# Expert work spread over the quads of a recurrent scan by a table of shares instead of evenly

## The reference, cut to what matters

```python
def step(h, inp):                      # branch s: a scan over 1024 steps
    dAt, dBt, xt, Ct = inp
    h = dAt * h + dBt * xt[..., None]
    h_norm = jnp.sqrt(jnp.sum(h * h, axis=(1, 2), keepdims=True))
    scale = jnp.minimum(20.0 / (h_norm + 1e-08), 1.0)
    h = h * scale
    y = jnp.einsum('bdn,bn->bd', h, Ct) + Dp * xt
    return (h, y)
...
exp_batches = jnp.einsum('tec,td->ecd', sec_mask, xt)      # branch f: 8 experts, top 2 of 8, 1280 slots each
h = jax.nn.gelu(jnp.einsum('ecd,edf->ecf', exp_batches, c_fc), approximate=False)
exp_out = jnp.einsum('ecf,efd->ecd', h, c_proj)
out = cb_weight.reshape(T, N_EXP * cap) @ exp_out.reshape(N_EXP * cap, d)
```

## Time and profile before

| | |
|---|---|
| median of 3 runs | 1628.38 us (1627.27 to 1630.05) |
| the profiled execution: its own time | 1631.96 us |
| its span in the profile | 1630.2 us |
| busy: PE, DVE, ACT, POOL | 79%, 93%, 71%, 47% |
| mean granted TensorE clock | 0.892 |
| expert work runs in | about 304 to 1420 us of the span |

### The profile page before, as it was taken

The page is one execution under the profiler, slowest core; times in us unless marked ns, Lnnn a source line. Parts: engine busy times, 40 slices in busy tenths (PEclk is TensorE's granted clock), DMA queues, the critical chain, the costliest instruction groups (busy, mean ns, idle before and its releaser), DMA issues.

```text
span 1630.2 us, 34378 instructions
## 1 busy us (share of the span) xinstructions
PE 1280.4 (79%) x9628; PEld 1121.2 (69%) x9628; DVE 1519.3 (93%) x9635; ACT 1161.4 (71%) x2944; POOL 770.5 (47%) x1254
## 2 busy tenths in 40 slices
PE   5665535689899888989989997999989798945661
PEld 4555434578788777878878786888878688734550
DVE  6888888999999999999999999999999999987788
ACT  7887647577786868777776877778777767846550
POOL 4267767444444443444443344344444434468852
PEclk9767767799999999999989999999999999978795
DMA  9921111201120020120012002101201100012255
GB/s 342 320 74 48 46 41 43 96 18 30 38 73 24 18 74 24 37 74 24 24 42 69 17 30 67 37 31 35 64 16 28 66 28 18 18 42 71 72 160 186
DMA packets 85088, 104.56 MB, mean 64 GB/s; under 512 B 7712, under 2 KB 75936, under 8 KB 84896
## 3 DMA queue, kind: packets, MB, share of 16 engines
q1 hardware_dynamic: 76848, 85.47, 16.2%
q0 software_dynamic: 6144, 16.79, 3.2%
q10 hardware_dynamic: 1904, 0.09, 0.1%
HBM read 56.45 MB, written 45.88 MB: 63 GB/s over the span
## 4 chain that ended last, share of the span: by engine, by line
PE 49%; POOL 15%; ACT 15%; DVE 11%; issue 8%; DMA 2%; POOLq 0%; SPq 0%; ACTq 0%; DVEq 0%
PE ps L1277 16%; PE ps L1261 13%; PE ps L1249 8%; POOL arena L520 7%; PE ps L1243 5%; POOL xg L503 4%; ACT arena L891 4%; PE ps L1211 2%; DVE arena L694 2%; ACT arena L1008 2%; DVE arena L720 2%; DVE arena L740 2%; POOL wf L509 2%; DVE arena L730 2%; POOL wp L509 2%
## 5 line engine op out<-in xcount | busy, mean ns | idle before, releaser
L520 POOL TENSOR_TENSOR arena<-arena,neghalf 128x1 f32<-128x1 f32 x1025 | 594.6, 580 | 791.5 <-DVE arena L684 786.7
L694 DVE SCALAR_TENSOR_TENSOR arena<-arena 128x128 f32<-128x128 f32 x1024 | 363.4, 355 | 23.3 <-POOL arena L520 23.3
L1249 PE MATMUL ps<-arena,pick 128*128 128x128 f32 x2048 | 299.9, 293 | 63.2 <-ACT arena L1008 39.7
L1249 PEld LDWEIGHTS ps<-arena,pick 128*128 128x128 f32 x2048 | 276.5, 209 | 77.1 <-ACT arena L1008 64.4
L1261 PE MATMUL ps<-arena,wf 128*128 128x256 f32 x1280 | 306.8, 391 | 22.5 <-ACT arena L1023 10.4
L1008 ACT ACTIVATE arena<-ps,arena 128x128 f32<-128x128 f32 x1024 | 292.3, 374 | 29.6 <-PE ps L1249 27.8
L1277 PE MATMUL ps<-wp,arena 128*128 128x256 f32 x1280 | 303.7, 392 | 9.0 <-ACT arena L1023 5.9
L730 DVE CUSTOM_DVE_ANT_0 arena<-arena 128x128 f32<-128x128 f32 x1024 | 293.0, 286 | 12.2 <-ACT arena L1008 8.9
L720 DVE CUSTOM_DVE_ANT_0 arena<-arena 128x128 f32<-128x128 f32 x1024 | 298.5, 291 | 2.2
L689 DVE TENSOR_TENSOR arena<-arena 128x128 f32<-128x128 f32 x1024 | 289.4, 283 | 0.0
L1261 PEld LDWEIGHTS ps<-arena,wf 128*128 128x128 f32 x1280 | 243.2, 197 | 54.9 <-ACT arena L1023 11.2
(11 more groups left out here) (148 smaller groups left out, 1329.1 us busy)
## 6 DMA issues: line engine op xcount, KB each, us to landing
xg<-zeros SPq DMA_DIRECT2D x10, 1024.0 KB, 10.9
xrow<-xg SPq DMA_DIRECT2D x40, 256.0 KB, 2.8
yg<-arena SPq DMA_DIRECT2D x40, 256.0 KB, 2.2
arena<-in_x SPq DMA_DIRECT2D x16, 512.0 KB, 9.1
wf<-in_c_fc SPq DMA_DIRECT2D x8, 1024.0 KB, 5.3
wp<-in_c_proj SPq DMA_DIRECT2D x8, 1024.0 KB, 6.1
ys<-arena SPq DMA_DIRECT2D x66, 64.0 KB, 1.6
xnd<-arena SPq DMA_DIRECT2D x8, 512.0 KB, 6.8
```

Source lines behind the costliest of these rows:

```text
L520: g.tensor_tensor(sv[:, slot, 1:2], mx, neghalf[:, 0:1], ALU.pow).then_inc(s_ready, 1)
L694: v.scalar_tensor_tensor(hr[:, slot, :], vv, sv[:, before, 1:2], ur[:, slot, :], ALU.mult, ALU.add).then_inc(h_ready, 1)
L1249: last = t.matmul(ps[2][:, j * P:(j + 1) * P], pick[:, q * QUAD + j, :], xin, start=True, stop=True)
```

## The change

Each quad from 41 to 229 gets a share ("room"): 0.8 in a half's last quad (15), 0.3 in its first (0), 0.7 in the second (1), 0.9 in the third (2) and fifth (4), and 1.0 elsewhere. The item list is the same, in the same order; an item goes to the first quad at which the accumulated room exceeds the item's middle, in units. The sixteen shares of a half add up to 14.6, so a quad of share 1.0 is meant to get 16/14.6 of the even load.

```diff
+import itertools
...
         QUADS, MOE_AT, MOE_QUADS, COMBINE_AT, LAST_HALF = NT // QUAD, 41, 230, 237, 240
+        share = {15: 0.8, 0: 0.3, 1: 0.7, 2: 0.9, 4: 0.9}
+        room = [share.get(qd % 16, 1.0) if MOE_AT <= qd < MOE_QUADS else 0.0 for qd in range(QUADS)]
+        ends = list(itertools.accumulate(room))
         n = 0
         total = sum(w[3] for w in work)
         by_quad = [[] for _ in range(QUADS)]
         for w in work:
-            by_quad[MOE_AT + (n + w[3] // 2) * (MOE_QUADS - MOE_AT) // total].append(w)
+            by_quad[next(qd for qd in range(QUADS) if ends[qd] > (n + w[3] / 2) / total * ends[-1])].append(w)
             n += w[3]
```

## The result

The changed kernel takes **1656.33 us** (1645.62 to 1657.55, five runs) against 1630.05 us (1627.27 to 1633.14) for the one before beside it: ratio 1.0154, 95% interval 1.0125 to 1.0183. It is slower, as forecast, but by 26 us where some 8 were forecast, and outside the range. The latter is called the longer profile, the former the shorter one.

What follows compares the result with a forecast made beforehand. VectorE's scan was taken as bound by a slower feeding chain of TensorE and ScalarE, 11.2 us of waits. Terms: -23.9 + 34.2 - 5.5 + 2.6 - 1.6 + 1.8 = +7.6 us on 1628.4, so 1636 us; range 1620 to 1644 us.

Steps and rivals of the forecast that it cites:

- The feeding chain: TensorE's matmuls for a quad, ScalarE's eviction, the next quad; feeds VectorE's scan, slower than it by 19.7 us.
- three stretches: Each half's last two, first two and other twelve quads, summed over halves 3 to 13: together 1038.3 us before.
- First two quads: Start of each half, 154 units to 80: down to ScalarE's floor, 189.2 to 165.3 us, -23.9.
- Last two quads: End of each half, 150 units to 151: -1.6 us against 160.4.
- a unit's price in busy time: A unit is the item list's weight; 0.444 us each, 77 more in the twelve quads +34.2 us.
- the twelve quads: Quads 2 to 13 of halves 3 to 13, bounded by TensorE: 925 units to 1002, from 688.8 to about 720 us.
- Rival (a): Faster: TensorE's gaps in the twelve quads swallow most of the moved work, 0.17 us a unit, 1620 us; chance 0.26.
- a quarter of the 22.6, -5.5: Twelve quads: a quarter of TensorE's 22.6 us of idle time there takes up moved work, -5.5 us.
- rival (c): Start of a half: TensorE idles a second time and its clock falls, +9 to +12 us, 1646 us; chance 0.1.
- The second idle time: TensorE waits up to 4 us for the second quad's L1008, the first quad being empty.
- the table loads, +2.6: Second to fourth quad: four more ScalarE table loads of 1.28 us, half of 5.1 us on the path.
- nearly every microsecond ... is a microsecond of the kernel: Lead is never large again after half 3, so changes to the stretches' sum change the kernel's time nearly one for one.

Runs made afterwards that it cites:

- longer profile: Profile of an execution of the changed kernel run again without any edit: 1657.13 us.
- shorter profile: Profile of the changed kernel's first measurement, the fastest of its five executions: 1645.62 us.
- e2_first_two: Kernel before with only the shares of a half's first and second quad (0.3 and 0.7): 1652.96 us, ratio 1.0131.
- e3_last: Kernel before with only the share of a half's last quad (0.8): 1632.15 us, ratio 1.001.
- e4_more_first: Kernel before with more work at a half's start, share 1.5 in its first quad and 1.3 in its second: 1650.12 us, ratio 1.0104.
- e12_less_work: Changed kernel with 76 units of expert work left out of quads 2 to 13 of halves 3 to 13: 1634.21 us, ratio 1.0026 to before.
- e7_one_table: Changed kernel with the Gelu's table, which holds tanh too, loaded after each half's Ln, 37 loads instead of 47: 1654.55 us, ratio 1.0144 to before.
- e11_other_three: Kernel before with only the shares of a half's last (0.8), third and fifth quad (0.9): 1625.37 us, ratio 0.9982.

## Why the prediction missed

**Right: the mechanism and two of its three stretches.** The feeding chain bounds, its sum of three stretches moves the time (12.2 us of sum for 13.7 of time in the first profile, 24.1 for 25.2 in the longer one), and the work went from quads where it is partly free to quads where TensorE is full. First two quads: forecast 165.3, measured 163.25 and 164.65. Half 5, forecast about 18, took 18.76, half 13, forecast 15.3, 14.45. Last two quads: forecast -1.6, measured -1.5 and +0.2. VectorE's waits for quads: forecast 19 in all, measured 23.5, most of them for a half's second quad, as forecast, and 34.6 in the longer profile.

**Right: a unit's price in busy time.** What the twelve quads gained or lost against before, in us, split into TensorE's busy time at full clock, the cost of the lower clock (half of the change of the busy time at 1.2 GHz) and idle time:

| run | units | stretch | busy, full clock | a unit | lower clock | idle |
|---|---|---|---|---|---|---|
| changed, shorter profile | +77 | +39.6 | +34.2 | 0.44 | +3.4 | +2.1 |
| changed, longer profile | +77 | +48.4 | +33.6 | 0.44 | +13.2 | +1.6 |
| e2_first_two | +53 | +31.1 | +23.6 | 0.44 | +5.7 | +1.8 |
| e3_last | +16 | +1.5 | +6.3 | 0.39 | -2.4 | -2.3 |
| e4_more_first | -41 | -8.8 | -16.5 | 0.40 | +3.3 | +4.4 |

The forecast was 34.2 for 77 units, and e12_less_work gives the same 0.44. Rival (a) fell with it. The Trainium skill, "Perfetto Trace Analysis", section "Identifying the Most-Contended Engine", would judge TensorE's headroom by weight loads (and by the share of its peak rate), not by matmul busy time. Weight loads were busy 629.5 of 728.4 us, 86%, and the trace disagrees with the rule here: a unit cost its full price all the same. What is added to the price, or taken off, is clock and idle time: in e3_last both fell, and 16 units more lengthened the stretch by only 1.5 us.

**Wrong: "a quarter of the 22.6, -5.5".** Idle time in the twelve quads went from 22.6 to 24.7 and 24.2 us. The prediction read the gaps as mostly those behind quads with little work, where ScalarE is slower. By what ended it, the idle time before is 11.7 us for the copy of the transposed inputs (L952), 3.8 for the late weight load, 3.5 for ScalarE's input terms (L1008), 2.7 for nothing that the profile shows and 0.9 for the copy of turned rows (L1027). Only the 3.5 are of the kind that the prediction meant. They were filled, down to 0.8 in the longer profile; the first two and the fourth stayed (11.4, 3.9, 2.7). New ones came in their place: 3.0 us in which a "down" waits for a Gelu, and 2.2 instead of 0.9 for the copy of turned rows.

**Wrong: the clock priced as rival (c), chance 0.1, "at 2.9 us in three or four halves".** It is part of the usual execution. The second idle time was seen, but expected where an "up" alone stands in the second quad (halves 4, 7, 9). It came in 7 and 9, not in 4, and also in halves 8 and 11, with a "down" there, and 12, with two "up"s, since with the first quad empty ScalarE's chain ended after TensorE's work there too. The lower clock in the twelve quads costs 3.4 us more than before in the shorter profile and 13.2 in the longer one, whose time the other runs share (1654 to 1658 us). The prediction's sum has no term for it. The twelve quads, forecast +31.3 with the table loads: in the longer profile 34.2 for units, 13.2 for the clock and 1.6 of idle time make 49.0, measured 48.4. The two failed terms, 13.2 and 5.5 + 1.6, are 20.3 us; the change cost 26.3 us against 7.6 forecast, 18.7 more.

**Mis-sized: the table loads, +2.6.** e7_one_table puts ten loads at 2.0 us, so four at about 0.8, an estimate. The Trainium skill, "ScalarE: Activation LUTs", section "What ACT_TABLE_LOAD costs", would give ten switches an estimated 26.6 us of ScalarE's time. The trace agrees with its figure for the load, 1.28 us, but shows no drain: ScalarE stood idle 0.02 us before a load and 0.01 us behind it (medians of the 47 in the longer profile).

**Only half right: "nearly every microsecond ... is a microsecond of the kernel".** Upward it held: at the start of half 15, behind all expert work, the two profiled executions of the changed kernel are 11.7 and 23.5 us behind before's, for sums that are 12.2 and 24.1 longer. Downward 3 to 5 us were lost on the way: e11_other_three cut the sum by 11.8 us and its execution is 8.8 ahead at that point, e3_last by 8.7 and is 3.7 ahead. e3_last's execution (1636.14 us) then loses 7.7 us in half 15, as e7_one_table's loses 7.5, most of it in waits for L1215 (7.0 and 6.8 us from 1455 us on; none before); why some executions do was not tried. Whether lead gained early in a half is lost later was not tried either.

**Smaller slips in the prediction's numbers.** A quarter of 22.6 is 5.65. The two stretches compared in rival (a) differ by 0.86 us in length and 1.07 in idle time, not by 0.69. The granted clock in the first two quads of before goes up to 0.91, not 0.83. The units don't balance: 74 leave the first two quads and 82 arrive elsewhere, as 8 more leave quads 222 to 229 (57 to 49), for which the sum has no term. And the list has 280 items, seven for each of 40 tiles, not 360; the 1320 units are right.

## What to carry to other kernels

Work that is moved from a place where an engine idles to one where it is full costs its full price in busy time there. Before gaps are counted on to take it up, sort them by what ends them: here most waited for things that the move didn't touch. And the place that is left can cost too: here TensorE idled there and its clock fell behind it. A slow spell in a stretch that another engine bounds was hidden; the same spell a few microseconds later was not. Look first for what a waiting engine needn't wait for (the eviction ahead of Exp, 8.2 us for one moved call), before work is shifted by shares.

## What was not expected of the hardware

One program, without any change, took 1645.6 and 1654 to 1658 us, 0.7% apart. In the two executions that were profiled, 8.8 of the 11.5 us between them lie in the twelve quads, with 19.6 us more of busy time at 1.2 GHz: idle times of 2.92 and 1.63 us at the same place of half 8 were followed by a "down" of 5.62 and of 3.62 us. In the shorter execution the clock had come back later, within the part that ScalarE bounds.
